# Two-layer transformer block on one core: quotients by exp(-log) and a Newton step, with other places for scatters, turns and loads

## The reference, cut to what matters

```python
q = elu(q) + 1; k = elu(k) + 1
kv_cumsum = cumsum(k * v, axis=tokens)
k_cumsum = cumsum(k, axis=tokens)
out = q * kv_cumsum / (q * k_cumsum + 1e-9)      # this quotient is the edited one
```

## Time and profile before

| | before |
|---|---|
| median of three runs | 913.24 us (911.77 to 915.14) |
| the profiled execution | 915.11 us, of which the span of the profile is 913.3 |
| PE busy | 781.7 us, 86% |
| DVE busy | 617.8 us, 68% |
| ACT busy | 476.8 us, 52% |
| POOL busy | 217.6 us, 24% |

### The profile page before, as it was taken

The page is one execution under the profiler, slowest core; times in us unless marked ns, Lnnn a source line. Parts: engine busy times, 40 slices in busy tenths (PEclk is TensorE's granted clock), DMA queues, the critical chain, the costliest instruction groups (busy, mean ns, idle before and its releaser), DMA issues.

```text
span 913.3 us, 13644 instructions
## 1 busy us (share of the span) xinstructions
PE 781.7 (86%) x4873; PEld 378.7 (41%) x4878; DVE 617.8 (68%) x1189; ACT 476.8 (52%) x991; POOL 217.6 (24%) x329
## 2 busy tenths in 40 slices
PE   3466756896687999999999999999999999879895
PEld 1243433452232444445444544454454444323343
DVE  5999998537764677576666766766766677797222
ACT  2355312864054656565665656555655656555561
POOL 2838775205730000000000000000000000770012
PEclk9789777997688999999999999999999999998998
DMA  9703031244328036325323532532352241350011
GB/s 301 258 1 104 14 137 46 70 163 145 125 87 136 3 108 136 80 76 117 89 65 91 116 89 82 112 117 65 81 119 71 76 116 39 94 185 1 12 36 47
DMA packets 78102, 86.98 MB, mean 95 GB/s; under 512 B 34390, under 2 KB 61513, under 8 KB 77641
## 3 DMA queue, kind: packets, MB, share of 16 engines
q1 hardware_dynamic: 72216, 74.84, 30.0%
q0 software_dynamic: 3328, 9.38, 3.3%
q10 hardware_dynamic: 2488, 1.89, 0.7%
HBM read 40.34 MB, written 28.31 MB: 75 GB/s over the span
## 4 chain that ended last, share of the span: by engine, by line
PE 59%; DVE 14%; issue 8%; POOL 7%; ACT 7%; DMA 3%; ACTq 1%; SPq 1%; POOLq 0%; DVEq 0%
PE bank L1523 13%; PE bank L1501 10%; PE bank L1481 9%; PE bank L1449 7%; PE bank L1459 5%; PE bank L1538 3%; POOL x_rows L579 3%; DVE PR L970 3%; PE bank L1317 3%; POOL XT L590 3%; DMA OPS<-qk_parts 2%; PE bank L1360 2%; ACT PR L820 2%; PE bank L1566 2%; DVE ACC L874 2%
## 5 line engine op out<-in xcount | busy, mean ns | idle before, releaser
L1216 DVE TENSOR_REDUCE PM<-bank 128x1 f32<-128x512 f32 (+3 forms) x640 | 363.8, 604 | 180.4 <-PE bank L1484 143.1
L820 ACT ACTIVATE PR<-bank 128x512 f32<-128x512 f32 (+3 forms) x640 | 328.3, 534 | 277.5 <-PE bank L1501 157.5
L1481 PE MATMUL bank<-OPS 108*128 108x512 bf16 (+3 forms) x640 | 229.3, 364 | 11.9 <-DVE PM L1216 5.1
L1501 PE MATMUL bank<-OPS 111*128 111x512 bf16 (+3 forms) x640 | 225.0, 355 | 12.8 <-ACT PR L820 9.6
L1523 PE MATMUL bank<-PR,VS 128*17 128x512 f32 (+3 forms) x1280 | 155.9, 539 | 2.4 <-ACT PR L820 0.4
L555 POOL TENSOR_TENSOR NP<-NM,NIL 128x8 bf16<-128x8 f32 x32 | 7.8, 244 | 503.9 <-DVE NM L1224 503.8
L1481 PEld LDWEIGHTS bank<-OPS 108*128 108x128 bf16 x640 | 64.7, 101 | 95.1 <-DVE PM L1216 64.3
L1501 PEld LDWEIGHTS bank<-OPS 111*128 111x128 bf16 x640 | 62.6, 98 | 89.0 <-ACT PR L820 66.8
L1449 PE MATMUL bank<-WB 128*128 128x256 f16 x552 | 91.0, 273 | 1.0
L1449 PEld LDWEIGHTS bank<-WB 128*128 128x128 f16 x552 | 47.8, 100 | 42.2 <-issue 21.2
L1484 PE MATMUL bank<-MASK 128*128 128x128 bf16 x256 | 58.6, 229 | 0.0
(11 more groups left out here) (177 smaller groups left out, 888.5 us busy)
## 6 DMA issues: line engine op xcount, KB each, us to landing
WB<-W SPq DMA_DIRECT2D x23, 512.0 KB, 3.6
x_rows<-PR SPq DMA_DIRECT2D x23, 256.0 KB, 3.9
WB<-in_w SPq DMA_DIRECT2D x23, 256.0 KB, 3.4
y_rows<-XT SPq DMA_DIRECT2D x23, 256.0 KB, 3.0
OPS<-qk_parts SPq DMA_DIRECT2D x28, 192.0 KB
OPS<-qk_parts SPq DMA_DIRECT2D x28, 128.0 KB
W<-in_w SPq DMA_DIRECT2D x6, 512.0 KB, 5.4
qk_parts<-WB SPq DMA_DIRECT2D x8, 384.0 KB, 2.9
```

Of the source, the lines that this page charges most:

```text
L820: act.activation(PR[:, tile % RING, off:CH], PS[2 + tile % 2][:, off:CH], ACT.Exp).then_inc(b_exped, 1)
L1216: dve.tensor_reduce(PM[:, c % 2, j, xq, gg:gg + 1], bank[:, 0:width], AX.X, ALU.max).then_inc(a_reduced, 1)
L1481: last = mm(bank[:, 0:width], OPS[0:ROWS_A, h % 4, 0, P * (TC * a + xq):P * (TC * a + xq) + P], OPS[0:ROWS_A, h % 4, 1, CH * gg:CH * gg + ...
L1501: last = mm(bank[:, off:CH], OPS[0:ROWS_B, h % 4, 1, P * k:P * k + P], OPS[0:ROWS_B, h % 4, 0, CH * b + off:CH * b + CH], start=True, stop ...
```

## The change

- Layer 0's quotients. ACT computes U = exp(-log(DEN)) in four activations per chunk, placed between its front(c+1) and the other work ahead of back(c). DVE multiplies DEN by U, then makes (DEN*U - 2) * U, which is minus the reciprocal after one step of Newton's rule, and the last product takes NUM * -1 * that. The reciprocal is gone.
- Turns. The first pair's TURN_AT go from steps 12, 28, 52, 84 to 24, 40, 58, 84. Later pairs keep theirs.
- Scatters. The groups between POOL's first maxima were 4, 5, 7 and 0 tiles; they are now 3, 3, 5 and 5.
- Loads. first_load(c) follows the stores of its own chunk instead of those of the next. SP no longer waits for the scatters before load(2) and load(3).

```diff
-TURN_AT = {chunk_end(m) - 1 + 5: m for m in range(NC * PAIRS)}
+TURN_AT = {chunk_end(m) - 1 + (17, 17, 11, 5)[m] if m < NC else chunk_end(m) - 1 + 5: m for m in range(NC * PAIRS)}
...
-                if c:
-                    first_load(c - 1)
-            first_load(NC - 1)
+                first_load(c)
...
-            sp.wait_ge(x_scattered, 16 * 2 * NT)
             load(2)
             load(3)
...
-            scatter(range(0, 4))
+            scatter(range(0, 3))
             maxima(0)
-            scatter(range(4, 9))
+            scatter(range(3, 6))
             maxima(1)
-            scatter(range(9, NT))
+            scatter(range(6, 11))
             maxima(2)
+            scatter(range(11, NT))
             maxima(3)
...
+            def first_reciprocal(c):
+
+                for m in range(2):
+                    act.wait_ge(nd2, 2 * c + m + 1)
+                    if c:
+                        act.wait_ge(rcp, 4 * c - 2 + 2 * m)
+                    act.activation(U[:, m, :], DEN[:, m, :], ACT.Ln).then_inc(rcp_log, 1)
+                for m in range(2):
+                    act.wait_ge(rcp_log, 2 * c + m + 1)
+                    act.activation(U[:, m, :], U[:, m, :], ACT.Exp, scale=-1.0).then_inc(rcp_first, 1)
...
                 front(c + 1)
+                first_reciprocal(c)
...
+            first_reciprocal(NC - 1)
             back(NC - 1)
...
                 for m in range(2):
-                    wait(dve, nd2, 2 * c + m + 1)
-                    dve.reciprocal(DEN[:, m, :], DEN[:, m, :]).then_inc(rcp, 1)
-                    wait(dve, rcp, 2 * c + m + 1)
+                    dve.wait_ge(rcp_first, 2 * c + m + 1)
+                    dve.tensor_tensor(DEN[:, m, :], DEN[:, m, :], U[:, m, :], ALU.mult).then_inc(rcp, 1)
+                    dve.wait_ge(rcp, 4 * c + 2 * m + 1)
+                    dve.scalar_tensor_tensor(DEN[:, m, :], DEN[:, m, :], 2.0, U[:, m, :], ALU.subtract, ALU.mult).then_inc(rcp, 1)
+                    dve.wait_ge(rcp, 4 * c + 2 * m + 2)
                     wait(dve, numden, 2 * c + m + 1)
                     wait(dve, s_ps, 2 * c)
-                    dve.tensor_tensor(OT0[:, m, :], NUM[:, m, :], DEN[:, m, :], ALU.mult).then_inc(outT, 1)
+                    dve.scalar_tensor_tensor(OT0[:, m, :], NUM[:, m, :], -1.0, DEN[:, m, :], ALU.mult, ALU.mult).then_inc(outT, 1)
```

More of the change, by code:

```diff
@@ L284, in build @@
         bias_part, bias_in = sem("bias_part"), sem("bias_in")
+        rcp_first, rcp_log = sem("rcp_first"), sem("rcp_log")
         rows_made, ranked = sem("rows_made"), sem("ranked")
```

## The result

| | median us | range | runs |
|---|---|---|---|
| before | 912.5 | 911.46 to 915.14 | 4 |
| changed | 890.81 | 888.55 to 891.25 | 4 |

The ratio is 0.9753, with a 95% interval from 0.9726 to 0.9781: 21.7 us faster, against 24.7 forecast, and 2.3 us above the forecast time. The profiled execution took 891.25, span 889.4.

A forecast was written before the change was run, and what follows sets the result against it. It took DVE's order of work to bound layer 0, waits for POOL's NP and heads 2 and 3 the entry, PE the rest. Entry 17.7 + layer 0 7 = 24.7 us off 913.24 gave 888.5; range 882 to 893.

The forecast's parts named there:

- The three holes: Entry into layer 1's attention: DVE's two holes (2.5 + 5.3 us) and PE's third wait for NP (2.8) close.
- The loads: Entry: loads of heads 2 and 3 land at 265, before step 80; 4.9 us of wait and 2.2 of clock saved.
- Block 0: Entry: fetch_block(0) follows all scatters, SP goes on at 262.1, data there at 279; slack 3.6 us, no stall.
- (b): Rival, entry: loads and scatters collide, the pair of heads needs 36 us or more or block 0 is late; 896, chance 0.13.
- The entry's sum: Entry into layer 1's attention: 2.5 + 5.3 + 2.8 + 4.9 + 2.2 = 17.7 us saved, bounds 12 to 20.
- Layer 0's sum: Layer 0: about 0, 3, 2 and 2 us saved in chunks 0 to 3, sum 7, bounds 1 to 13.
- Table loads: Layer 0, ACT: two loads of 1.28 us taken per chunk, for Ln and, behind it, Tanh; none to three thought possible.
- POOL's stretch: Layer 0, DVE: operations with two SBUF operands take some 0.74 us more than 0.69 where POOL runs.
- (a): Rival, layer 0: ACT eats the gain, Tanh and L1360 come as late as before; saves 0 to 1, 895, chance 0.17.
- (c): Rival, layer 0 and entry: everything hides, layer 0 gives 13 and the entry 20; 880, chance 0.08.
- (d): Rival, layer 0: each table load costs several times 1.28 us; at 4 us 6.7 slower, 920, chance 0.02.
- (e): Rival, entry: the holes only move to the new turns; 888.5 + 10.7 = 899, chance 0.03.

The follow-up runs named there:

- after: The changed kernel's first trace, nothing else edited: profiled execution 891.25 us, median 890.81 us.
- e10: The changed kernel, unedited, run again beside the kernel before on a chip without stalls: 891.1 us, ratio 0.9742.
- e13: The changed kernel with the last pair's turns at 5, 17, 11 and 5 tiles behind the chunks' ends instead of 5 each: 884.13 us, ratio 0.9692.
- before: The first trace of the kernel without the change: profiled execution 915.11 us, span 913.3.
- e9: The kernel without the change, unedited, run again on a chip without stalls: 911.89 us, ratio 0.9988.
- e2: The kernel without the change, given only the new layer 0 quotients (Ln, Exp, Newton step): 923.09 us, ratio 0.9948.
- e3: The kernel without the change, given only the later turns and smaller scatter groups: 928.48 us, ratio 1.0022.
- e12: The changed kernel without its 32 scatters of x_rows and the two waits for them: 892.61 us, ratio 0.9786.
- e6: The changed kernel with ACT's position rows moved from chunks 0 and 1 to chunks 2 and 3: 911.81 us, ratio 0.9867.
- e7: The changed kernel with the last pair's turns at 5, 17, 11 and 5 tiles behind the chunks' ends: 908.23 us, ratio 0.9852.

## Why the prediction was right, point by point

The time, 890.81 for 888.5, lies in the range, and the likeliest case came. That it came within 2.3 us is in part luck: by the traces the change is worth 20.6 us, not 24.7. By its steps:

- **The three holes** ("So the three holes close"): shown in `after` and e10. No wait for NP in the entry, DVE without a hole.
- **The loads** (landing at 265, ahead of step 80 at 272.8, both less layer 0's 7): shown. Step 80 came at 263.6, with no wait for them and the clock at 1.00 from 245 us.
- **Block 0** (SP goes on at 262.1, slack 3.6): no stall, but by two errors that cancelled. SP went on at 258.1, 3.4 later than 262.1 less layer 0's 7.4. POOL was not late: it issued its last scatter at 251.9, but this one had landed only 6.2 us later, for 2.4 in the earlier trace rows. In e10 and e13 it is 6.3 us too. That fits the loads that now run beside the scatters, rival (b) in small; no run isolates it. Against that the transposing transfer landed 3.4 us after its issue, for 11.9 in the earlier trace rows, so that the slack was 8.7 us. The price of 11.9 was not the transfer's own: in `before`, e9, e2, e3 and e12, where it goes out some 6 us behind the last issue of heads 2 and 3, its issue alone takes 7.4 to 7.6 us; in the other nine traces, where the distance is 10 us or more, 1.4.
- **The entry's sum**, 17.7: measured 19.3 in the first pair of traces, 19.1 in the second. The excess fits the clock: 1.00 from 250 us on, where before it was 0.80 from 250 to 265 and 0.77 from 280 to 295.
- **Layer 0's sum**, 7: the first pair shows 7.4, but that is luck; the term was too large by 2.8. Over the five traces with reciprocals the first A tile starts at 213.6 us on the mean (211.8 to 217.3), over the six with the change's layer 0 as it is at 209.4 (208.7 to 210.0): 4.2 us. The first trace of before was the extreme. Most of what it has over e9 (3.5 of 4.9 us at the last output projection) is one group of DVE. Its timeline there, ahead of the last quotients:
```profile
134.83 6.36 DVE L874 TENSOR_SCALAR ACC<-XO,MV,RSTD 128x256 f32<-128x256 f32 x4
```
and in e9:
```profile
132.84 2.83 DVE L874 TENSOR_SCALAR ACC<-XO,MV,RSTD 128x256 f32<-128x256 f32 x4
```
By chunks, `after` against before, and e10 against e9: the first L1374 1.9 and 1.6 us later (0 predicted); the way to the second 5.5 and 5.1 shorter (3); to the third 1.5 and 1.5 shorter (2); to the fourth 2.3 shorter and 1.7 longer (2). Chunk 1 earned more: none of its new operations was stretched. Chunk 3 earned 0.3 on the mean. Its time hangs on the group above more than on the edit: the four operations took 6.36, 2.83, 1.95 and 6.06 us in `before`, e9, `after` and e10, each time with POOL at work. In `after`, DVE then stood 2.49 us for U and had four stretched operations; in e10 it had no wait and two.
- **Table loads**: eight, as forecast, but ahead of Ln and of Exp, so DVE's quotients wait behind them (1.26 us in chunk 0 and 2.49 in chunk 3), and Tanh needs none of its own. The row also decides between the two prices: the activation before the load ends at 51.97, the load starts at 51.99 and the next activation at 53.28, so a switch is 1.28 us and no more. The Trainium skill (ScalarE: Activation LUTs, What ACT_TABLE_LOAD costs) has 2.66 us for a switch, of which 1.28 are the load, as here, and the rest a drain, which the trace doesn't show. By the table of the Trainium skill (ScalarE: Activation LUTs, Table sets: the hidden batching unit), ln and then exp need one load; the trace has two.
- **POOL's stretch** (0.74 us each): the eight operations under POOL in `after` took 1.23 to 2.50, 0.97 more than 0.69 on the mean for the 0.74 expected. Their number was as expected, though none fell in chunk 1 and four in chunk 3. The mechanism was right, the size low. The Trainium skill's sentence (GPSIMD Engine Reference, Specifications) on the shared interfaces is borne out, 0.69 alone against up to 2.50.
- **The step that failed** (it cost 2.8 us of the forecast): "After 300 us PE sets the pace and nothing there is edited, so what is won ahead of it is kept to the end." From step 92 to the end the changed kernel takes 616.0 and 617.4 us, before 613.2 and 614.6: 2.8 us given back in both pairs, the term that lacked in the sum. The waits of PE are the same (2.7 to 3.0 us for the NP behind the last gathers); what grew is the time at half clock behind it: by windows of 1 us 6.8 us in each trace of before, and 10.2 in each of the change. In the first pair of traces the lead goes from 27.4 to 25.7 us there, which is half of the 3.4 us, as work at half clock takes twice its time. It goes from 25.7 to 23.9 behind 867 us, where the stretches at half clock are longer too (12.5 us for 8.5). Why the same pause is followed by 7 or by 10 us at half clock isn't settled: e12 has the change's turns and 6.8. e13 shows what removes the first stretch: not turning before POOL can be ready.

The sum of the means, 19.2 + 4.2 - 2.8 = 20.6 us, stands against 21.7 between the first medians, and on the chip of e9 and e10 against 20.8 or 23.3, by which of the two sets of runs of the kernel before is taken (911.89 or 914.4). So 1 to 3 us stay unassigned.

Of the rivals, (a) is true for chunk 0 alone, (b) cost the 3.4 us above and no stall, (c) came in the entry (19.2 of its 20) and not in layer 0, and (d) and (e) didn't come. Of the four signs of being wrong none came: the gate waits for Tanh in chunk 0 alone, DVE's new operations average 1.05 us, and neither block 0 nor the loads of heads 2 and 3 stop PE.

## What to carry to other kernels

Two edits that remove two waits ending close together can each be worth nothing alone and, here, 7.4 us together by the medians (19 in the traces without stalls); time them together before dropping one. An instruction that only prepares (a turn of maxima) should be placed by when the slow engine's queue lets its producer run: where POOL has sixteen gathers in front of it, six steps later cost nothing, and the last pair's new turns gave 5 to 7 us. And a won microsecond is not kept by itself: a pause of 3 us late in the kernel was paid twice, as a pause and as 6.8 to 10.2 us at half clock behind it.

## What the runs showed of the hardware

- The same program has a different time by chip: 912.5, 914.4 and 913.4 us in three groups, 927 and 924 on the chips of two others, there with pauses of 9 to 22 us on DVE in the entry that the profile ascribes to nothing. On one of the latter the change with e6's or e7's small edits was worth 1.3 to 1.5%, on the former the change alone 2.5 to 2.6%.
- A pause of PE of 2.7 to 3.0 us at an otherwise dense stretch was followed by 6.8 to 10.2 us at 1.2 GHz, in five traces.
- 128x512 operations of DVE with two operands in SBUF took 0.69 us alone and up to 2.50 beside POOL; the four of L874 or L886 on 128x256 took from 1.95 to 6.36 us in one place of four traces, with POOL at work in each.
- The transposing transfer of block 0 took 3.3 to 4.9 us from issue to landing in nine traces and 11.6 to 11.9 in four in which it went out some 6 us behind the last issue of heads 2 and 3.
- Leaving out 32 scatters made the changed kernel no faster (ratio 0.9786, against 0.9742 and 0.9753 with them): block 0's transfers then go out right behind the loads of heads 2 and 3.
